# Slot columns and head weights moved to GpSimd, a re-ordered tail, and matrix products into an unread buffer

## What is computed

```python
h = conv(sign(x), sign(kernel)) + bias; h = (h - mean) * rsqrt(var + eps) + beta      # x: (4, 750, 128), h: (4, 748, 64)
qkv = layernorm(h) @ Wqkv + bqkv;  q, k, v = reshape(qkv, (3, b, n, d, heads=8))
attn = softmax(einsum('bnqh,btqh->bnth', q, k) / 8, axis=1)
h = h + einsum('bnnh,bnqh->bnqh', attn, v).reshape(b, n, 512) @ W0 + b0              # only the diagonal of attn is used
x2 = layernorm(h); current = 0
for level in range(8):                                                              # 255 nodes, 128 leaves
    score = x2 . w1s[current] + b1s[current]
    out += (x2 @ w2s[current] + b2s[current]) * gelu(|score|)
    current = 2 * current + (score > 0) + 1
h = h + out
```

## Time and profile before

| | |
|---|---|
| median of 3 runs (all) | 474.37 us (473.8, 474.37, 483.96) |
| profiled execution, its own time | 474.62 us |
| its span (first to last instruction) | 472.7 us |
| mean granted TensorE clock | 0.911 |
| busy: PE, DVE, ACT, POOL (GpSimd) | 352.7, 342.5, 324.0, 284.2 us |

### The profile page before, as it was taken

One profiled execution on the slowest core, in us unless ns is written; L12 is line 12 of the kernel. 1 busy time (PEld: TensorE's weight loads), 2 busy tenths in 40 slices (PEclk: granted clock), 3 DMA queues, 4 the chain that ended last, 5 costly groups with the idle time before them and its releaser, 6 DMA issues.

```text
span 472.7 us, 8346 instructions
## 1 busy us (share of the span) xinstructions
PE 352.7 (75%) x2606; PEld 248.5 (53%) x2606; DVE 342.5 (72%) x577; ACT 324.0 (69%) x832; POOL 284.2 (60%) x398
## 2 busy tenths in 40 slices
PE   1156896878789889777898769883512999999970
PEld 1144565655456555445664446552312777788860
DVE  0475969899788878998888998978530789955440
ACT  1363996788888998577898656758200799987760
POOL 4315748786867875584689662661552365666663
PEclk9996999989999999989999999995555999999995
DMA  4425243417998972131243130018915012120000
GB/s 95 128 62 136 53 113 81 101 39 172 178 187 160 151 182 47 53 97 29 71 113 97 38 82 1 3 42 116 118 31 139 23 36 56 33 54 6 12 15 5
DMA packets 58953, 37.27 MB, mean 79 GB/s; under 512 B 31661, under 2 KB 57607, under 8 KB 58906
## 3 DMA queue, kind: packets, MB, share of 16 engines
q1 hardware_dynamic: 54778, 33.81, 35.7%
q0 software_dynamic: 3328, 2.36, 2.0%
q10 hardware_dynamic: 800, 0.49, 0.5%
HBM read 11.42 MB, written 7.50 MB: 40 GB/s over the span
## 4 chain that ended last, share of the span: by engine, by line
DVE 33%; issue 17%; ACT 15%; PE 15%; POOL 12%; DMA 5%; SPq 1%; POOLq 0%; DVEq 0%; ACTq 0%
DVE nm L1392 14%; ACT Z L1192 10%; POOL out L726 8%; PE Z L923 6%; POOL pre L723 3%; DMA pre<-in_x 3%; DVE va L1421 2%; ACT q L1134 2%; DVE pre L1488 2%; ACT k L1134 1%; PE Z L843 1%; DMA pool_a<-pool_a 1%; DVE pre L1503 1%; DVE va L1437 1%; DVE pre L1665 1%
## 5 line engine op out<-in xcount | busy, mean ns | idle before, releaser
L1192 ACT ACTIVATE Z<-Z,nm 125x748 f32<-125x748 f32 x192 | 166.3, 872 | 61.5 <-DVE nm L1392 60.2
L1392 DVE TENSOR_REDUCE nm<-Z 125x1 f32<-125x748 f32 x192 | 175.4, 933 | 36.4 <-PE Z L923 30.0
L923 PE MATMUL Z<-pool_a 128*125 128x512 f16 (+1 forms) x768 | 162.0, 338 | 28.1 <-ACT Z L1192 23.4
L923 PEld LDWEIGHTS Z<-pool_a 128*125 128x125 f16 x768 | 87.7, 140 | 71.8 <-ACT Z L1192 46.0
L726 POOL DMA_INDIRECT out<-pre,va x44 | 44.7, 1017 | 35.1 <-POOL pre L723 35.1
L1665 DVE TENSOR_REDUCE pre<-va 128x64 f32<-128x512 f32 x44 | 45.7, 1039 | 5.8 <-ACT va L1275 2.4
L790 PE MATMUL Z<-xhT,wq 128*128 128x249 f16 (+1 forms) x192 | 32.9, 291 | 11.9 <-DVEq L1402 10.5
L1192 ACT ACTIVATION_READ_ACCUMULATOR Z<-Z,nm 125x1 f32 x192 | 41.2, 215 | 0.0
L652 POOL DMA_INDIRECT sorted_rows<-xrow,slot x24 | 30.4, 1266 | 15.3 <-DVE slot L1544 8.7
L620 POOL TENSOR_TENSOR va<-va 125x256 f32<-125x256 f32 (+2 forms) x54 | 29.6, 548 | 10.3 <-DVE va L1421 7.2
L596 POOL TENSOR_TENSOR pool_a<-q,pool_a 128x748 f16<-128x748 f32 x15 | 24.7, 1644 | 10.2 <-DVE pool_a L1349 9.1
(11 more groups left out here) (243 smaller groups left out, 667.1 us busy)
## 6 DMA issues: line engine op xcount, KB each, us to landing
pool_a<-pool_a SPq DMA_DIRECT2D x64, 187.0 KB, 3.3
pool_a<-pool_a SPq DMA_DIRECT2D x64, 93.5 KB, 2.2
sorted_rows<-zrow SPq DMA_DIRECT2D x1, 3640.0 KB, 23.8
va<-sorted_rows SPq DMA_DIRECT2D x12, 260.0 KB, 3.0
w<-in_L_ffn_w2s SPq DMA_DIRECT2D x1, 2048.0 KB, 16.5
pre<-in_x SPq DMA_DIRECT2D x4, 375.0 KB
pool_a<-in_L_ffn_w2s SPq DMA_DIRECT2D x1, 1024.0 KB
out<-pre,va POOLq DMA_INDIRECT x44, 2.2
```

Source lines behind the costliest of these rows:

```text
L923: last = mm(z[0:XP, c0:c1], kst[:, u % 3, a, hd, KST[t]:KST[t] + XP], qst[:, u % 3, hd, c0:c1], start=(a == 0), stop=(a == 1))
L1192: sc_.activation(z, z, ACT.Exp, bias=nm[0:XP, u % 4, i:i + 1], accum_out=sm[0:XP, u % 4, i:i + 1]).then_inc(s_exp, 1)
L1392: v.tensor_reduce(nm[0:XP, u % 4, i:i + 1], Z[n % 3][0:XP, 0:N], X, ALU.max, negate=True).then_inc(s_max, 1)
```

## The change

It has five parts.

1. **Weights.** For units 0 to 11 DVE only inverts the sums; GpSimd multiplies (`weights(u - 1)`, behind `qk_lo(u + 2)` and a piece of zeroing), and `weigh_heads` waits for it.
2. **Slot columns** of batches 0 and 1 go to GpSimd: `leaf_terms` (units 9, 13), `group_terms` (10, 14), `slot_terms` (11, 15), 15, 8 and 10 instructions. DVE keeps two short functions that copy out of PSUM.
3. **Zeroing** of the leaf table: five pieces in units 5 to 9; the DMA of its bias row is issued in unit 13 instead of 7.
4. **Tail.** The first two pairs of batch 3 are weighed together (`yq`, 512 wide, three times); the last diagonal goes to `Z[0]` without a fill's bank; `leaf_counts(2)` comes behind the layer norm of batch 3, its normalised rows before the ranks, `slots(2)` behind the node logits of batch 3; the low table's columns come behind the last scatter.
5. **Tiles.** 84 products of constants into `Z[1]`, which nobody reads, between PE's register loads (12 instead of 16) and in front of the first rows; GpSimd adds the residual of tile k + 1 before it writes tile k; for overflow tiles DVE adds it.

```diff
             if 1 <= u < NU and i < 3:
                 f.append(("d", u - 1, i))
...
+                f += {7: [("yq", 0)], 9: [("yq", 1)], 11: [("yq", 2)]}.get(i, [])
...
-                f += {(0, 8): [("A", b - 1, 0)], (0, 10): [("A", b - 1, 1)], (1, 10): [("pf", b - 1)],
-                      (2, 9): [("sl", b - 1)]}.get((ph, i), [])
+                f += {(0, 8): [("A", b - 1, 0)], (0, 10): [("A", b - 1, 1)], (2, 2): [("pf", b - 1)],
+                      (3, 2): [("sl", b - 1)]}.get((ph, i), [])
...
+            def weights(w):
+                pool.wait_ge(s_rc, w + 1)
+                pool.wait_ge(s_ex, w + 1)
+                gp.tensor_tensor(at[0:XP, w % 8], at[0:XP, w % 8], sm[0:XP, w % 4], ALU.mult).then_inc(s_atp, 1)
...
+                if ZERO_AT <= u < ZERO_AT + ZPARTS:
+                    pool.wait_ge(s_prod, u + AHEAD + 1)
+                    leaf_zeros(u - ZERO_AT)
...
+                if 1 <= u <= LASTB:
+                    weights(u - 1)
+                if 1 <= b < B - 1 and ph == 1:
+                    leaf_terms(b - 1)
+                if 1 <= b < B - 1 and ph == 2:
+                    group_terms(b - 1)
                 if 0 <= b < B - 1 and ph < 2:
                     for t in range(3 * ph, 3 * ph + 3):
                         add_heads(b, t)
...
                 if b >= 1 and ph == 3 and b < B - 1:
+                    slot_terms(b - 1)
                     own_slots(b - 1)
...
             own_slots(B - 2)
+            own_slots(B - 1)
             pool.wait_ge(s_zl, LOWZ)
             low_columns()
-            own_slots(B - 1)
...
+            residual(0)
             for k in range(ST_TILES):
+                if k + 1 < ST_TILES:
+                    residual(k + 1)
                 rows_out(k)
...
+            for k in range(ST_TILES, ST_TILES + EARLY):
+                early.append(load_leaves(k))
+                for n in range(3):
+                    keep_awake()
...
             def weigh_heads(b, t):
-                dve.wait_ge(s_at, NPAIR * (b + 1))
+                dve.wait_ge(s_atp, NPAIR * (b + 1))
...
                         ln2_last()
+                        leaf_counts(B - 2)
+                        old_terms()
+                        ln2_last_x()
                         rank_of_token(B - 2)
```

More of the change, by code:

```diff
@@ L243, in fills @@
             f = []
-            if 1 <= u <= NU and i < 3:
+            if 1 <= u < NU and i < 3:
                 f.append(("d", u - 1, i))
@@ new lines, in group_terms @@
+            def group_terms(b):
+                pool.wait_ge(s_gc, b + 1)
+                link(gp.tensor_tensor(col[:, c_new], col[:, c_new], col[:, c_cap], ALU.subtract))
+                link(gp.tensor_tensor(leaf[:, 4:5], col[:, c_last], col[:, c_j32], ALU.subtract))
+                link(gp.tensor_tensor(leaf[:, 5:6], col[:, c_new], col[:, c_last], ALU.subtract))
+                if b:
+                    pool.wait_ge(*full(("sl", b - 1)))
+                link(gp.tensor_copy(leaf16[:, 0, :], leaf[:]))
+                gp.tensor_tensor(leaf16[:, 1, :], leaf[:], leaf16[:, 0, :], ALU.subtract).then_inc(s_vn, 1)
+                pool.wait_ge(s_vn, b + 1)
+                link(gp.tensor_scalar(col[:, c_up], col[:, c_dn], 0.0, 1.0, ALU.is_gt, ALU.mult))
+                link(gp.tensor_tensor(col[:, c_up], col[:, c_up], leaf[:, 5:6], ALU.mult))
+                link(gp.tensor_tensor(col[:, c_last], col[:, c_last], col[:, c_up], ALU.add))
@@ new lines, in slot_terms @@
+            def slot_terms(b):
+                bt = slice(b * NT, (b + 1) * NT)
+                pool.wait_ge(s_sc, b + 1)
+                e, z = beyond[0:XP], slz[0:XP]
+                for n in range(2):
+                    link(gp.tensor_tensor(e[:, :, n], z[:, :, 0], z[:, :, 2 + n], ALU.subtract))
+                    link(gp.tensor_scalar(e[:, :, n], e[:, :, n], 0.0, 1.0, ALU.is_ge, ALU.mult))
+                    link(gp.tensor_tensor(e[:, :, n], e[:, :, n], z[:, :, 4 + n], ALU.mult))
+                link(gp.tensor_tensor(slf[0:XP], z[:, :, 1], e[:, :, 0], ALU.add))
+                for n in range(1, 3):
+                    link(gp.tensor_tensor(slf[0:XP], slf[0:XP], e[:, :, n], ALU.add))
+                gp.tensor_copy(slot[0:XP, bt], slf[0:XP]).then_inc(s_slot, 1)
@@ L857, in pair_out, with two_pairs_out @@
                     last = mm(zt, pick[:, g, 0:XP], cb[:, js], start=False, stop=True)
+                last.then_inc(s_full, 1)
+            def two_pairs_out(n):
+                z = take(("yq", n))
+                for t in range(2 * n, 2 * n + 2):
+                    r0, g = v_tile(B - 1, t)
+                    zt = z[0:XP, t % 2 * 2 * P:(t % 2 + 1) * 2 * P]
+                    for a in range(2):
+                        mm(zt, xhT[:, r0:r0 + XP], mw[:, a, g * H * D:g * H * D + 2 * P], start=(a == 0), stop=False)
+                    last = mm(zt, pick[:, g, 0:XP], cb[:, 0:2 * P], start=False, stop=True)
                 last.then_inc(s_full, 1)
@@ L934, in fill @@
                     heads_out(f[1], f[2])
+                elif kind == "yq":
+                    two_pairs_out(f[1])
                 elif kind == "yp":
@@ L1068, in _, with keep_awake @@
             pe.wait_ge(s_goff, 1)
-            early = [load_leaves(k) for k in range(ST_TILES, ST_TILES + EARLY)]
+            def keep_awake():
+                mm(Z[1][:, 0:LEAVES], tri[:], pathb[:], start=True, stop=True)
+                mm(Z[1][:, 512:512 + LEAVES], tri[:], pathb[:], start=True, stop=True)
+            early = []
+            for k in range(ST_TILES, ST_TILES + EARLY):
+                early.append(load_leaves(k))
+                for n in range(3):
+                    keep_awake()
+            pe.wait_ge(s_tab, 16 * 2)
+            pe.wait_ge(s_low, 16 * 2 * sum(2 ** (lvs[-1] - lv) for _, lvs in LOW for lv in lvs))
+            pe.wait_ge(s_wc, 2)
+            pe.wait_ge(s_zl, LOWZ + 1)
+            for n in range(6):
+                keep_awake()
             xs_T(0)
@@ L1555, in take @@
                     weigh_heads(f[1], f[2])
+                elif kind == "yq":
+                    weigh_two(f[1])
                 elif kind == "yp":
```

204 lines of the change are left out of this document (145 added, 59 removed).

## The result

The changed kernel is slower: 493.28 us (median of four, 489.74 to 496.04) against 475.46 for the kernel before; the ratio is 1.0353, 95% interval 1.0285 to 1.042. The forecast was 479.5 and its range ended at 490. The profiled execution took 495.95, its span is 494.2. From here on "changed" is that kernel. Times are medians of all executions of a kernel, while ratios and their intervals leave out executions more than 1.5% above the fastest of the same kernel.

The account below looks back on a forecast made before the run. No engine was taken as the bound: the ring of three buffers limits the loop, so a wait on DVE is lost one for one. 474.6 + 12.3 - 1.6 - 1.5 - 4.0 = 479.8, given as 479.5; range 464 to 490.

Parts of the forecast that it names:

- the likeliest case: Whole kernel: slower, at 479.5 us, its own range 474 to 485, chance 0.5.
- Waits for the weights: Loop, step 8 of units 4, 8 and 12: DVE waits for GpSimd's weights, 1.1, 4.7 and 7.7 us.
- Waits for the squares: Second layer norm, units 7 and 11: DVE waits for GpSimd's squares, 1.5 and 7.2 us.
- TensorE's clock: Loop: PE falls to half clock in the new waits and DVE then waits for it, 2.5 us lost.
- Unit 15 and batch 3: End of loop: joined addition delays PE's rows in unit 15, 2.5 us lost; fewer weighings, later fills, 1.5 saved.
- Savings: Loop: 9.2 us from slot columns off DVE, 4.2 from zeroing out of unit 1, 1.5 in batch 3; 14.9 together.
- Routing: After the loop: counts beside GpSimd's work and PE's slots of batch 2 behind the node logits save 1.6 us.
- Tiles, clock of the first: First tile: PE's first products at full clock instead of half, so it comes 1.5 us earlier.
- the third rival: Tiles: constant products between register loads end 5 us after the rows, time 486 us, chance 0.08.
- Output: End of the tiles: GpSimd keeps up with DVE, so the end after DVE's last sum saves 4.0 us.
- The second rival: Units 8 to 15: GpSimd becomes the bound, small instructions at 0.5 us instead of 0.28; 489 us, chance 0.17.

Follow-up runs that it names:

- e1: The changed kernel with the weights multiplied by DVE again in all units, directly behind the reciprocal: 475.43 us, 0.997 of the kernel before.
- e3: The changed kernel with GpSimd's weights of units 3, 7 and 11 moved ahead of its split and product in units 4, 8 and 12: 477.68 us.
- h2: The changed kernel once more, on the same chip as h3: 486.94 us.
- h3: The changed kernel with constant products given to PE in its waits of units 8, 11 and 12: 480.06 us.
- e2: The changed kernel with the slot columns of batches 0 and 1 back on DVE, the weights still on GpSimd: 494.98 us, 1.0355 of the kernel before.
- e4: The changed kernel without the constant products, the 12 register loads kept: 493.74 us, 1.0323 of the kernel before.
- i1: The kernel of h1 with GpSimd's group_terms and squares ahead of its split and product in unit 10 alone: 469.09 us, 0.9887 of the kernel before.
- i2: The kernel of e1 (weights on DVE, new output) once more, beside i3: 467.64 us, 0.9845 of the kernel before.
- i3: The kernel of h1 (weights on DVE, output as in the kernel before) once more, beside i2: 471.61 us, 0.9912 of the kernel before.
- i4: The kernel before once more, one execution for a second profile: 472.03 us.
- j2: The kernel before once more, one execution for a third profile: 475.75 us.
- g2: The kernel of e1 with the static tiles' old output order, the overflow tiles' residual still on DVE: 476.49 us, 0.9985 of the kernel before.
- h1: The kernel of e1 with the whole output as in the kernel before: 472.66 us, 0.991 of the kernel before.

## Why the prediction was wrong

The sign of the likeliest case was right, its size was not: 495.95 against 479.8, 16 us more.

- *Waits for the weights* (1.1, 4.7, 7.7): 0.88, 4.61, 8.60. Right, by the rows that the prediction named. e1 and e3 show that the order on GpSimd is their cause.
- *Waits for the squares* (1.5, 7.2): 1.33, 5.64. Right, a little long. In e1 1.04 and 5.39.
- *TensorE's clock*: "0 to 6, I take 2.5". This is the step that failed: the mechanism was right, its price too small. Keeping the clock up in the waits of units 8, 11 and 12 alone gave back 6.9 us by the medians of h2 and h3, beyond the upper end. The prediction knew that three waits would be long enough for a fall. The fall before was, as it read it, hidden mostly by DVE's queue, and it took the new ones as partly hidden too; but in the changed kernel DVE stood 1.72 us for PE twice between the weighings of unit 8, and these came 4.85 apart instead of 3.46. That it was dearer because DVE had lost its slot work is not shown, and e2, where DVE has it back, speaks against it: from the reciprocal of unit 8 to that of unit 9 took 28.0 us there, which is the 21.5 of before, the wait of 4.62 and 1.9 more; from unit 12 to unit 13 it is 30.5, which is 21.7, the wait of 5.61 and 3.2 more. What the kernel before paid for its own fall at 208 us was not measured, so the term against that kernel may be smaller by as much.
- *Unit 15 and batch 3* (+2.5 and -1.5): from the reciprocal in unit 14 to the end of the last maximum 27.7 us, 22.7 before: +5.0 where +1.0 was forecast. In e1 it is 26.5, so this isn't the weights; in e4, i1, i2 and i3 it is 24.9, so 2.2 of the 5.0 come every time and the rest by execution. The second step that failed; which of its parts (the joined addition, the later fills, the half clock) it is was not tried apart.
- *Savings* (14.9): right for the slot columns, short for the rest. From unit 8 to 10 and from 12 to 14 e1 took 2.8 and 5.5 us less than the kernel before, where 3.7 and 3.7 of the 9.2 were to fall. Zeroing: units 1 to 4 took 53.5 us instead of 56.4 in the changed kernel, 2.9 of the 4.2, but 55.6 in e1 and from 53.5 to 58.2 in the other profiles that have it. The 1.5 of batch 3 lie in the row above and don't show.
- *Routing* (-1.6): right. From the end of the last maximum to the first scatter of batch 3 it is 32.1 us, 34.2 before (33.7 in i4 and j2).
- *Tiles, clock of the first* (-1.5): nothing that shows. The loads and products end 2.5 us before the rows come, not after them as the third rival had it, and in the changed kernel the half clock only moved to 385 to 388 us, behind the first rows' products.
- *Output* (-4.0): right. 4.0 by the medians of i2 and i3, on a chip without pauses, and the end after DVE's last instruction fell from 6.1 to 1.8; that the medians meet the forecast to the tenth is luck, since i2's four executions spread over 3.9. In the profiled execution of the changed kernel pauses in the static tiles took 6.9. The prediction had no term for them, since no row of before shows one.

Of the 16 us that were missing, the loop has 10 (by these terms clock 4 to 6, its end 4, zeroing 1, less 1 for the waits) and the pauses 7; the rest cancels. The forecast 479.5 is also 0.3 below its own sum, without a reason. The second rival, which ended at 489, had more half clock in it, but its ground was another, slower small instructions on GpSimd; these kept their 0.28 (0.25 to 0.35 from one to the next in `group_terms`), and no wait was longer than forecast by more than 0.9.

What stays open: what the pauses are. They showed in all eight profiles taken on two of the chips, every one with at least a part of the new output (in g2 only in the overflow tiles), and in the changed kernel's first one; in none of the ten of old or new output on two others. h1, with the wholly old output, never ran where others paused, and the kernel before's times are alike on all chips (476.98, 476.44, 477.11, 476.62, 477.47), so that the new output has a part in them is likely, not shown. Instructions being loaded is a rival that the trace speaks against: in the changed kernel's profile the queues that carry instructions moved nothing from 407 to 416 and from 417 to 428 us, and the two pauses shown above lie there; in g2's nothing from 440 to 452.

## What to carry to other kernels

Before a small operation is moved to an engine with slack, look at what stands ahead of it in that engine's list at the moment when its result is wanted: the same twelve instructions cost 18 us behind a product and 2 when three of them stood ahead of it. But look also at what an instruction moved ahead pushes back: the squares ahead of the split gained in unit 10 and lost in unit 6. Price a wait twice, once for its length and once for the PE steps behind it at half clock, and don't count on the waiting engine's other work to hide these: in e2 it had such work and the stretches behind the waits were still 1.9 and 3.2 us longer. A gain at the end of a kernel can be real and not show on one chip, so compare both kernels on the same one.

## What the runs showed of the hardware

- Products into a bank about to be overwritten kept the granted clock at 1.00 through waits of 4.7 to 8.7 us (h3), and gave back 6.9 us in a kernel whose waits they hardly shortened.
- Products that ended 2.5 us before the real work didn't keep it at full clock: the clock was 1.00 to 384 us, 0.50 from 385 to 388 and full again behind that (changed kernel), and no time was gained.
- In eight profiles on two chips PE and ACT paused in the tiles with no engine of this core to wait for (ACT 1.6 to 3.8 us in the rows shown, up to 11.4 us between two sums); in ten on two others they didn't, the changed kernel's among them: 493.28 and 486.94 us.
